# Last stage of a routed-experts kernel: who computes the inverse root, and who adds the second expert rows

## What is computed

```python
x = x + _layernorm(_L0_attn_ref(_layernorm(x), ...))
# experts: combined = sum of the two chosen experts' rows, each times its weight; shared_out = the shared expert
return_of_ffn = (combined + shared_out).reshape(B0, S0, H0)
x = x + _layernorm(return_of_ffn)      # (v - mean) / sqrt(var + 1e-5) over 128 channels
```

## Time and profile before

| | us |
|---|---|
| median of 3 runs | 247.47 |
| lowest, highest | 245.0, 247.66 |
| the profiled execution, its time | 245.01 |
| its span in the trace | 242.9 |
| TensorE busy, share of the span | 223.1, 92% |
| VectorE | 167.0, 69% |
| ScalarE | 134.8, 56% |
| GpSimd | 162.1, 67% |
| mean granted TensorE clock | 0.977 |

### The profile page before, as it was taken

One profiled execution on the slowest core, in us unless ns is written; L12 is line 12 of the kernel. 1 busy time (PEld: TensorE's weight loads), 2 busy tenths in 40 slices (PEclk: granted clock), 3 DMA queues, 4 the chain that ended last, 5 costly groups with the idle time before them and its releaser, 6 DMA issues.

```text
span 242.9 us, 5859 instructions
## 1 busy us (share of the span) xinstructions
PE 223.1 (92%) x1270; PEld 160.9 (66%) x1270; DVE 167.0 (69%) x796; ACT 134.8 (56%) x502; POOL 162.1 (67%) x210
## 2 busy tenths in 40 slices
PE   7999887889999979999799999999999999989970
PEld 2868574545545335368688888888888888887340
DVE  3967989787999998868555656656655555511795
ACT  2848585474666753655455555555555555503761
POOL 7965757777777777777777666666665766660730
PEclk9999998879999999999999999999999999999996
DMA  6799001111111113641233233323233232108963
GB/s 178 201 316 275 0 22 49 56 56 45 57 60 45 57 56 91 166 125 58 78 98 106 81 100 88 93 69 110 69 99 80 81 89 78 47 22 280 395 235 131
DMA packets 28315, 26.34 MB, mean 108 GB/s; under 512 B 7014, under 2 KB 22259, under 8 KB 28288
## 3 DMA queue, kind: packets, MB, share of 16 engines
q1 hardware_dynamic: 22448, 15.38, 22.7%
q0 software_dynamic: 4320, 8.53, 9.9%
q10 hardware_dynamic: 1520, 2.10, 2.4%
HBM read 14.77 MB, written 11.68 MB: 109 GB/s over the span
## 4 chain that ended last, share of the span: by engine, by line
PE 69%; DVE 13%; DMA 5%; ACT 4%; issue 3%; POOL 2%; POOLq 1%; SPq 0%; ACTq 0%; DVEq 0%
PE bank L1388 12%; PE bank L1279 9%; PE bank L1361 6%; PE bank L1363 6%; PE bank L1362 6%; PE bank L1379 6%; PE bank L1149 4%; PE bank L1342 3%; PE bank L1291 3%; PE bank L1253 3%; PE bank L1165 2%; DMA xnT<-expert_results 2%; PE bank L1207 2%; ACT work L603 2%; DVE X L1136 2%
## 5 line engine op out<-in xcount | busy, mean ns | idle before, releaser
L545 POOL DMA_INDIRECT expert_results<-eo,rowt x71 | 69.8, 983 | 32.0 <-issue 29.2
L527 POOL DMA_INDIRECT expert_rows<-src,slot x64 | 63.4, 991 | 21.2 <-issue 18.6
L722 ACT ACTIVATE work<-bank 128x256 f32<-128x256 f32 x71 | 27.3, 384 | 46.0 <-PE bank L1363 45.9
L1388 PE MATMUL bank<-down,work 128*128 x284 | 44.1, 278 | 0.4 <-ACT work L729 0.2
L1085 DVE TENSOR_TENSOR work<-work,bank 128x256 f32<-128x256 f32 x48 | 20.2, 421 | 27.8 <-ACT work L722 27.2
L1388 PEld LDWEIGHTS bank<-down,work 128*128 128x128 f32 x284 | 37.3, 192 | 1.6 <-issue 0.8
L1361 PE MATMUL bank<-gu_hi,rh 128*128 x71 | 34.3, 484 | 0.3 <-DVE rl L1077 0.3
L1279 PE MATMUL bank<-xT,gu_f 128*128 128x512 f32 x64 | 33.5, 646 | 0.0
L729 ACT ACTIVATE work<-bank 128x256 f32<-128x256 f32 x71 | 27.8, 392 | 1.0 <-PE bank L1379 1.0
L1363 PE MATMUL bank<-gu_hi,rl 128*128 x71 | 28.1, 395 | 0.0
L1362 PE MATMUL bank<-gu_lo,rh 128*128 x71 | 27.9, 392 | 0.0
(11 more groups left out here) (195 smaller groups left out, 445.6 us busy)
## 6 DMA issues: line engine op xcount, KB each, us to landing
rowt<-expert_rows SPq DMA_DIRECT2D x71, 66.0 KB, 1.9
X<-n_L_attn_in_sequence_bwc SPq DMA_DIRECT2D x8, 256.0 KB, 3.9
X<-expert_results SPq DMA_DIRECT2D x8, 256.0 KB, 6.7
xnT<-expert_results ACTq DMA_DIRECT2D x8, 256.0 KB, 7.3
out<-X SPq DMA_DIRECT2D x7, 256.0 KB, 3.5
expert_results<-eo,rowt POOLq DMA_INDIRECT x71, 2.3
gu_f<-in_L_ffn_gate_proj_w SPq DMA_DIRECT2D x1, 1024.0 KB, 7.3
gu_f<-in_L_ffn_up_proj_w SPq DMA_DIRECT2D x1, 1024.0 KB, 10.0
```

What stands on the lines that cost most here:

```text
L527: nc.gpsimd.indirect_dma_start(rows_d, bass.IndirectOffsetOnAxis(ap=slot[i % SRC][:, n // TOPK, n % TOPK:n % TOPK + 1], axis=0), src[i % S ...
L545: nc.gpsimd.indirect_dma_start(res_d, bass.IndirectOffsetOnAxis(ap=rowt[v][:, P:P + 1].bitcast(U32), axis=0), eo[v][:], None, bounds_check ...
L722: nc.scalar.activation(sgate[v % 2], gu_ps[v % 2][:, 0:M], ACT.Silu).then_inc(slot_silu, 1)
L1388: last = mm(y_ps[w], hidT[w][:, a, :], down[:, e, a, :], start=a == 0, stop=a == MC - 1)
```

## The change

Four edits, all in the last stage:

- ROOT goes from 5 to 7: GpSimd computes the inverse root of units 0 to 6; the square root of ScalarE and the Newton step of VectorE are left for units 7 and 8 alone. Their five small instructions are spread between the scaling instructions of the unit before: `newton(m + 1, part)` stands behind tile i of unit m. The wait of ScalarE on `newton_c` is loosened in its wording, and no unit reaches it any more.
- VectorE adds the second rows of steps 0, 1, 2, 4 and 6 (BY_DVE), five instead of four; TensorE leaves out `add(n, second_y)` for unit 1.
- The stored shared rows are put into PSUM in transpose mode, not by a full matmul.
- The one-element square root of ScalarE, with the table load before it, moves ahead of the waits for the stores and ahead of its eight DMA issues.

```diff
-        ROOT = 5
+        ROOT = 7
+        BY_DVE = (0, 1, 2, 4, 6)
...
+            act.wait_ge(route_consts, 1)
+            nc.scalar.activation(table_in[:, 0:1], eps_col[:], ACT.Sqrt, scale=1.0)
             for v in range(UNROLL):
                 act.wait_ge(res_out[v], 16 * uses(v))
             for s in range(STEPS):
                 act.dma_start(tiles(second_y, s), res_v[:, 1, s * G:(s + 1) * G, :]).then_inc(y_in[s], 16)
-            act.wait_ge(route_consts, 1)
-            nc.scalar.activation(table_in[:, 0:1], eps_col[:], ACT.Sqrt, scale=1.0)
...
                 if n >= ROOT + 2:
-                    act.wait_ge(newton_c, (n - 1 - ROOT) * 4)
+                    act.wait_ge(newton_c, (n - 2 - ROOT) * 4 + 1)
...
+            def newton(m, part):
+                if not ROOT <= m < UNITS:
+                    return
+                u, count, at_c = m % 2, units[m][2], (m - ROOT) * 4
+                half, y, t = (x[:, 0:count] for x in (vpe[u][:, 1, :], guess[u], guess2[u]))
+                if part == 0:
+                    dve.wait_ge(sumsq4_done, m + 1)
+                    nc.vector.tensor_scalar(half, sumsq[u][:, 0:count], -0.5 / P, -0.5 * EPS, ALU.mult, ALU.add)
+                    dve.wait_ge(root_done, m - ROOT + 1)
+                    nc.vector.reciprocal(y, root[u][:, 0:count]).then_inc(newton_c, 1)
+                    return
+                dve.wait_ge(newton_c, at_c + part)
+                if part == 1:
+                    nc.vector.tensor_tensor(t, y, y, ALU.mult).then_inc(newton_c, 1)
+                elif part == 2:
+                    nc.vector.tensor_tensor(t, t, half, ALU.mult).then_inc(newton_c, 1)
+                else:
+                    nc.vector.scalar_tensor_tensor(out=rstd[u][:, 1, 0:count], in0=t, scalar=1.5, in1=y, op0=ALU.add,
+                                                   op1=ALU.mult).then_inc(newton_c, 1)
...
-                if n < STEPS and n % 2 == 0:
+                if n in BY_DVE:
                     dve.wait_ge(y_in[n], 16 * TOPK)
                     nc.vector.tensor_tensor(tiles(first_y, n), tiles(first_y, n), tiles(second_y, n),
                                             ALU.add).then_inc(z0_done, 1)
...
+                if m < ROOT:
+                    dve.wait_ge(ln4_c, m * 2 + 2)
+                else:
+                    dve.wait_ge(newton_c, (m - ROOT) * 4 + 4)
+                for i in range(count):
+                    last = nc.vector.scalar_tensor_tensor(...)
+                    if i == count - 1:
+                        last.then_inc(sum_done, 1)
                     else:
+                        for part in range(i, i + 1) if count == G else range(2):
+                            newton(m + 1, part)
+                for part in range(G - 1 if count == G else 2, G):
+                    newton(m + 1, part)
...
-                        mm(part, yshT[:, s, i * P:(i + 1) * P], ident[:], start=i == at, stop=False,
+                        mm(part, yshT[:, s, i * P:(i + 1) * P], ident[:], is_transpose=True, start=i == at, stop=False,
                            skip_group_check=True)
...
-                if s % 2 == 0:
-                    pe.wait_ge(z0_done, s // 2 + 1)
+                if n in BY_DVE:
+                    pe.wait_ge(z0_done, BY_DVE.index(n) + 1)
                 else:
                     pe.wait_ge(y_in[s], 16 * TOPK)
                     add(n, second_y, False, False)
```

More of the change, by code:

```diff
@@ L1109, in _ @@
                                             ALU.add).then_inc(z0_done, 1)
[L1110 to L1115, removed]
-                    else:
[L1118 to L1139, removed]
@@ new lines, in _ @@
+                if n < 3:
+                    continue
+                m = n - 3
+                s, at, count = units[m]
+                u = m % 2
+                if m < ROOT:
[3 more added lines that the diff above has]
+                for i in range(count):
+                    last = nc.vector.scalar_tensor_tensor(
+                        out=tile(first_y, s, at + i), in0=z_ps[m][:, i * P:(i + 1) * P],
+                        scalar=rstd[u][:, 1, i:i + 1], in1=tile(x1, s, at + i), op0=ALU.mult, op1=ALU.add)
+                    if i == count - 1:
+                        last.then_inc(sum_done, 1)
+                    else:
+                        for part in range(i, i + 1) if count == G else range(2):
+                            newton(m + 1, part)
```

## The result

The changed kernel is slower: median 248.68 us of 22 runs against 246.62 of 22 runs of the kernel before, ratio 1.0091 with a 95% interval of 1.0065 to 1.0117. The range of the forecast, 243.3 to 248.0, missed it. The profiled execution spans 244.8 us against 242.9, 1.9 more.

The account below looks back on a forecast made before the run. It took VectorE's last stage as the bound, set by unit 0's start at 227.04 and each unit's work after it. Net 1.64 − 0.85 = 0.8 us gained: 247.47 − 0.8 = 246.7 us, range 243.3 to 248.0.

Parts of the forecast that it names:

- GpSimd has no other work: Last stage, ROOT 5 to 7: GpSimd is free for units 5 and 6, 1.18 us gained in all by unit 6.
- stays at 2.9: End of the kernel: unit 8's two tiles and the last store still take 2.9 us after unit 8's start.
- Rival 4: Last stage: GpSimd, not VectorE, sets the pace; 247.5 us if VectorE's gain is eaten whole; chance 0.14 with slower GpSimd powers.
- The size of the Newton edits: Last stage, VectorE: ROOT 7 and spread Newton steps gain 1.64 us in all, bounds 1.1 and 1.9.
- 1.53 and 1.37 − 1.27: VectorE: 1.53 us gained in all by unit 7's start; units 7 to 8 take 1.27 us against 1.37.
- rival 2: GpSimd's added powers for units 5 and 6 take 1.47 us, not 1.01; 0.92 lost; chance 0.14 with gain eaten.
- the clock's fall: Last stage, TensorE: clock drops once to 1.2 GHz after a 3.0 us standstill, costing 0.85 us, bounds 0 and 1.7.
- The table load: ScalarE, last stage: moved into 9.77 us of idleness; nothing gained, at most 0.1 us.
- the fifth addition: VectorE adds step 1's second rows, 0.69 us where it idles; worth nothing while GpSimd's work on unit 0 hides it.
- the stretch that was named: TensorE, last stage: the clock falls once, between about 222 and 225 us.
- the two outcomes weighed: Clock falls once, 0.5 to 1.1 us gained, chance 0.53; clock holds, 1.4 to 1.9 gained, chance 0.28.
- its cover: GpSimd being busy on unit 0 until 227.01 us, which hides unit 1's squares ending 0.1 us earlier.

Follow-up runs that it names:

- the trace with two drains: The changed kernel with one GpSimd drain behind the scatter's 64 indirect DMAs and one behind the 71 stores; stage 20.9 us, single run 253.3 us.
- both losses taken away: The changed kernel with a GpSimd drain behind its last indirect DMA and full matmuls for the shared rows; stage 19.3 us, ratio to before 0.9975 (0.9921 to 1.0028).

## Why the prediction was wrong

**What was wrong.** The forecast gave 0.8 us gained; 2.06 were lost by the medians, 1.9 by the traces. VectorE's end did come forward, by 0.50. The step that failed is one half sentence, "GpSimd has no other work", and with it the assumption that the tail behind unit 8's start "stays at 2.9". The tail is the later of two: VectorE's last tile plus 2.3 us of store, and GpSimd's last power plus 7.9 us of drain. Before, the second was 2.0 us short of the first. The change moved GpSimd's last power from 231.88 to 235.71, by 3.8 us, and the first end forward by 0.5, so the second took over by 2.4. The page of the profile gave no sign of it; the closing code's row did, and I had not read it. Rival 4, GpSimd as the pace, named the right engine but priced only its powers, and stopped at nothing gained.

**What was right.** The size of the Newton edits: ROOT 7 with the steps spread moved VectorE's end by 1.69 and 1.57 us against 1.64 forecast (the prediction's own terms, 1.53 and 1.37 − 1.27, add up to 1.63, and rival 2 with the clock's fall comes to 247.6, not 247.5). Its split was not: it gave 1.18 to ROOT 7 and the rest to the spreading, but with ROOT 5 and the steps spread 1.3 is there already. Step by step in the changed kernel, unit 5 starts 1.42 after unit 4 (1.37 forecast), unit 6 1.26 after that (1.26), unit 7 1.50 (1.54), unit 8 1.24 (1.27). The table load and, as long as the clock holds, the fifth addition are worth nothing: with early drain and full matmuls VectorE ends at 17.0, with ROOT 7 alone at 16.8 and 16.9. The transposes end 2.8 us sooner, the clock falls in the stretch that was named, and of the two outcomes weighed the fall was held the likelier.

**Sizes that were off.** I took the clock's low stretch as 3.4 us after the one in the earlier trace rows. Of the seven traces with the change's transposes and the standstill, two show 3.4 us and five 6.8, the changed kernel among the five. In the changed kernel that cost less than assumed at unit 0 (0.52 instead of 0.9), because GpSimd's first power took 1.04 us there and not the 1.47 of the earlier trace rows. Why, the fourteen traces of this case tell together. In six of them that power starts while VectorE is still at an addition of 0.69 us, and takes 1.38 to 1.58 us, each time 1.04 plus the overlap less 0.14. In the eight without an overlap it takes 1.04. In three of these eight GpSimd's scaling instruction ahead of it starts beside an addition instead, and takes 0.64 to 0.67 us, not 0.20. Here the changed kernel, then ROOT 5 with full matmuls:

```profile
226.20 0.20 POOL L558 TENSOR_SCALAR vpe<-sumsq 128x4 f32<-128x4 f32 x1 [9.32 <-ACT work L753]
226.48 1.04 POOL L561 TENSOR_TENSOR rstd<-vpe,mhalf 128x4 f32<-128x4 f32 x1
```

```profile
228.52 0.69 DVE L1131 TENSOR_TENSOR X<-X,xnT 128x512 f32<-128x512 f32 x1 [0.98 <-DMA xnT<-expert_results]
228.63 0.64 POOL L558 TENSOR_SCALAR vpe<-sumsq 128x4 f32<-128x4 f32 x1 [8.38 <-ACT work L753]
229.35 1.04 POOL L561 TENSOR_TENSOR rstd<-vpe,mhalf 128x4 f32<-128x4 f32 x1
```

So the slow first power of rival 2 goes with an addition that runs beside it, which the late unit 0 escaped; the added powers of units 5 and 6 took 1.01.

Against the kernel without transposes the fall costs VectorE 0.7 to 1.0 us (17.0 against 17.7 and 18.0; forecast 0.85), 1.6 in the trace with two drains, all with the fifth addition; without it 1.7 and 2.3. I had that edit at nothing, or "0.1 gained" without its cover.

**The level.** The median was built on three runs at 247.47. With 22 the kernel before stands at 246.62, so the forecast's level was 0.85 too high beside the error in its sign. As a ratio it was 0.997, and 1.009 was measured. The trace of before has one more fall than the two that the prediction weighs, from 50.7 to 54.1, and TensorE was busy for 2.0 of the 3 us from 48 to 51 around its start; so a clock that fell in a thin stretch was there to be seen twice. The rule cited from the Trainium skill, "TensorE: Matmul & The Clock Gate", section "Why this matters for your kernels", agrees with the trace: the clock came down in a standstill of 3.55 us, where 3.0 was forecast, and in or up to 1.6 us after the standstills of the six other traces that have one, 3.1 to 3.9 us long.

**The account.** From 19.3 us with both losses taken away: the clock's fall adds 0.7 to 1.0 (20.0, 20.3), the closing drain 2.4 to 2.7 on top (22.7). The traces of these stages show it; the times can't resolve it. The kernel before is at 20.8. So the change holds a gain of 1.5 us and two losses of 3.4.

## What to carry to other kernels

A launch ends when every engine has arrived, and an engine's closing drain counts: before giving the last piece of work to an engine that has issued indirect DMAs, read its drain's row in the closing code, or put a drain where the engine idles after its last DMA. Test the parts of a change one by one: here the spreading had most of the gain, and ROOT 7 the loss. Time saved on an engine that then stands still can come back as a slow clock just when its critical work begins; the full matmuls that look wasteful here kept TensorE at 2.4 GHz, and with ROOT 5 the stage is 0.9 us shorter with them than with transposes.

## What the hardware showed that I had not expected

- GpSimd's first drain after indirect DMAs lasts 5.3 us beyond the last of 64, 5.9 beyond the last of 71 and 7.8 beyond the last of 135; a drain after that one takes no more than the instruction it waits for (1.1 us with a power of 1.0).
- Neither the busy times nor the chain of waits show it, and the wait for it (2.6 us) is put down to TensorE, whose drain was over 8 us earlier.
- GpSimd's power for unit 0 took 1.04 us by itself and 1.38 to 1.58 when it started beside an addition of VectorE (128x512 in float32); the addition took 0.69 either way.
- 48 float32 transposes in a row, 5.4 us, left TensorE's clock at 2.4 GHz (one trace).
